# Shared expert's down products five steps late, expert blocks in plain fp32 products, and a block loop turned two ahead

## The reference, cut to what matters

```python
xt = x.reshape(-1, D)                                   # 1568 x 256, layer-normed
gates = softmax(xt @ Wg.T); scores, inds = top_k(gates, 2)
h = silu(xt @ We_gate[e].T) * (xt @ We_up[e].T)         # 16 experts, hidden 128
y = sum over the token's two experts of score * (h @ We_down[e].T)
shared = silu(xt @ Ws_gate.T) * (xt @ Ws_up.T) @ Ws_down.T   # hidden 512
out = x + y + sigmoid(xt @ Wsg.T) * shared
```

## Time and profile before

| | us |
|---|---|
| median of 3 runs | 531.88 |
| the runs | 524.18 to 536.82 |
| profiled execution, its own span | 541.3 |
| PE busy in it | 398.8 (74%) |
| DVE, ACT, POOL busy | 336.6, 198.6, 149.2 |
| embedding, attention, gate scores (to 347.8) | 347.8 |
| shared expert on PE (347.8 to 434.9) | 87.1 |
| expert blocks on PE (434.9 to 516.3) | 81.4 |
| last scatters, sum and store (516.3 to 541.3) | 25.0 |

### The profile page before, as it was taken

One profiled execution on the slowest core, in us unless ns is written; L12 is line 12 of the kernel. 1 busy time (PEld: TensorE's weight loads), 2 busy tenths in 40 slices (PEclk: granted clock), 3 DMA queues, 4 the chain that ended last, 5 costly groups with the idle time before them and its releaser, 6 DMA issues.

```text
span 541.3 us, 11594 instructions
## 1 busy us (share of the span) xinstructions
PE 398.8 (74%) x3554; PEld 354.9 (66%) x3555; DVE 336.6 (62%) x962; ACT 198.6 (37%) x569; POOL 149.2 (28%) x209
## 2 busy tenths in 40 slices
PE   4777768788897878878778885568686877887910
PEld 5766657677786767767667664567676877876800
DVE  2888842637677777778687775672635644444537
ACT  4433354314243334334342222330422445555600
POOL 2534441011112121212111112066740015445420
PEclk9899969958798989899998886589898999889865
DMA  7323445532615161625435010482230004343247
GB/s 249 89 72 86 158 57 103 69 57 46 118 41 115 46 119 43 101 60 91 79 53 120 9 50 0 174 345 67 74 112 14 1 20 133 93 125 112 72 126 231
DMA packets 50985, 50.48 MB, mean 93 GB/s; under 512 B 30442, under 2 KB 43502, under 8 KB 50816
## 3 DMA queue, kind: packets, MB, share of 16 engines
q1 hardware_dynamic: 46080, 38.25, 29.8%
q0 software_dynamic: 4864, 11.71, 7.0%
HBM read 23.59 MB, written 15.34 MB: 72 GB/s over the span
## 4 chain that ended last, share of the span: by engine, by line
issue 44%; PE 15%; DVE 12%; SPq 7%; POOL 6%; DMA 5%; another core or an unknown queue 5%; ACT 4%; POOLq 1%; DVEq 0%; ACTq 0%
PE bank L1081 8%; SPq L455 5%; PE pair L1081 2%; DMA Ks<-parts 2%; POOL picked L582 2%; POOL sq L535 2%; PE bank L1243 1%; DVE h L1071 1%; DMA wg_sb<-wg 1%; DMA picked<-by,bx 1%; DMA yt<-picked 1%; DVE h L1069 1%; ACT we_h L710 1%; DVE hs L1027 1%
## 5 line engine op out<-in xcount | busy, mean ns | idle before, releaser
L1167 PE MATMUL pair<-vx,PT 98*128 98x128 f32 x512 | 82.2, 311 | 32.4 <-DVE on L893 32.3
L1167 PEld LDWEIGHTS pair<-vx,PT 98*128 98x128 f32 x512 | 73.1, 220 | 37.6 <-ACT PT L668 29.8
L870 DVE TENSOR_REDUCE smax<-bank 128x8 f32<-128x392 f32 x64 | 36.0, 562 | 52.4 <-PE bank L1147 51.6
L582 POOL DMA_INDIRECT picked<-by,bx x40 | 39.3, 983 | 79.9 <-ACT by L752 63.3
L668 ACT ACTIVATE PT<-bank 98x512 f32<-98x512 f32 x64 | 38.2, 597 | 62.0 <-PE bank L1156 60.0
L535 POOL TENSOR_TENSOR sq<-att 128x256 f32<-128x256 f32 x16 | 9.7, 609 | 160.1 <-DVE att L903 160.1
L1156 PE MATMUL bank<-cs,Sm 128*98 128x128 f32 x256 | 44.6, 302 | 0.0
L576 POOL DMA_INDIRECT slots_x<-hn2x,slot_u x32 | 34.3, 1073 | 27.4 <-DVE slot_u L1001 17.9
L1092 PE MATMUL bank<-wt_h,x_h 128*98 128x256 f32 x96 | 29.9, 311 | 10.9 <-DVE wt_l L762 6.8
L1048 DVE TENSOR_TENSOR bxT_l<-bank,bxT_h 128x256 fp32r<-128x256 f32 x40 | 17.0, 425 | 30.3 <-ACT bxT_h L735 24.2
L877 DVE TENSOR_TENSOR Sm<-bank,smax 128x392 f32<-128x392 f32 x64 | 35.0, 548 | 1.2
(11 more groups left out here) (188 smaller groups left out, 1162.0 us busy)
## 6 DMA issues: line engine op xcount, KB each, us to landing
we_raw<-we SPq DMA_DIRECT2D x12, 512.0 KB, 7.3
slots_x<-pad POOLq DMA_DIRECT2D x8, 642.5 KB, 6.5
bx<-slots_x SPq DMA_DIRECT2D x40, 128.5 KB
xr<-xt SPq DMA_DIRECT2D x16, 294.0 KB, 2.8
Qs<-parts SPq DMA_DIRECT2D x96, 49.0 KB
Ks<-parts SPq DMA_DIRECT2D x96, 49.0 KB
vx<-vst SPq DMA_DIRECT2D x64, 52.1 KB
yt<-picked SPq DMA_DIRECT2D x16, 196.0 KB
```

What stands on the lines that cost most here:

```text
L582: G.indirect_dma_start(out=picked, out_offset=bass.IndirectOffsetOnAxis(ap=bx[b % BX][:].bitcast(U32)[:, D:ROW], axis=0), in_=by[b % 4][:] ...
L870: V.tensor_reduce(smax[b][:], s3, AX.X, ALU.max).then_inc(maxed, 1)
L1167: last = T.matmul(bank[4 + b][:, m * 2 * VN:(m + 1) * 2 * VN].rearrange("p (j n) -> p j n", j=2), PT[b][:, m, :], vx[n][:, :, h0:h0 + VN], ...
```

## The change

The shared expert is no longer cut in chunks. `shared_expert` runs 16 steps u (chunk u//4, quarter u%4) on every engine: gate and up of u, then the down product of tile u-5; five more steps do the last downs. `hs_h` and `hs_l` are double. The experts' weights are not split: they are loaded into `we_sb` and used as fp32, and so are the turned rows (`bxT`, 4 buffers) and `bhT`. A block's gate/up is then 2 plain fp32 matmuls of 256 columns instead of 6 fp32r ones, its down product 1 instead of 3. Rows are turned two blocks ahead instead of one. The copy of the result (`block_keep`) moves from ACT to DVE; `by` has eight buffers. POOL copies the row numbers to a small tile (`keep_id`) four blocks ahead of the scatter, and SP reloads a `bx` buffer as soon as its rows are turned and its numbers kept. PE's wait for all `sh_acc` ahead of the blocks becomes a wait in the first two `block_hturn`.

```diff
+        DOWN_LAG = 5
+        NU = NSH * SB
...
-            pipeline(eng, steps, NBLK, BX, 1, 2, BX, begin)
+            pipeline(eng, steps, NBLK, BX, 2, 2, BX, begin)
+
+        def shared_expert(eng, gate_up, down):
+            for u in range(NU + DOWN_LAG):
+                if u < NU:
+                    gate_up(u // SB, u % SB, u)
+                if u >= DOWN_LAG:
+                    down(u - DOWN_LAG)
...
             def load_block(b):
                 if b >= BX:
-                    sp.wait_ge(by_out[b % 4], 16 * ((b - BX) // 4 + 1))
+                    sp.wait_ge(b_turned, b - BX + 1)
+                    sp.wait_ge(id_kept, b - BX + 1)
...
+            pool.wait_ge(sh_u, NU)
+            def keep_id(b):
+                q = b % BX
+                pool.wait_ge(bx_in[q], 16 * (b // BX + 1))
+                need(pool, by_out[q], 16 * (b // BX))
+                G.tensor_copy(bid[q][:], bx[q][:].bitcast(U32)[:, D:ROW]).then_inc(id_kept, 1)
+            ID_LEAD = 4
...
             for b in range(NBLK):
+                if b + ID_LEAD < NBLK:
+                    keep_id(b + ID_LEAD)
...
-            def split_expert(n):
-                act.wait_ge(we_in[n], 16)
-                A.activation(we_h[:, n * STG:(n + 1) * STG], we_raw[:, n * STG:(n + 1) * STG], ACT.Copy).then_inc(w_hi, 1)
...
-            blocks(act, [(1, block_hi), (0, block_silu), (-1, block_hhi), (-2, block_keep)])
+            blocks(act, [(2, block_xT), (0, block_silu), (-1, block_hT)])
...
+            def block_keep(b, q):
+                dve.wait_ge(b_y, b + 1)
+                need(dve, by_out[q], 2 * b - 2 * q)
+                V.tensor_copy(by[q][:], bank[6 + q % 2][:, 0:D]).then_inc(b_ykept, 1)
+            blocks(dve, [(0, block_h), (-2, block_keep)])
...
+            def shared_down(t):
+                c, tt = divmod(t, SB)
+                pe.wait_ge(sh_lo, SB * c + SB)
+                need(pe, sh_acc, t - 1)
...
             def block_gu(b, q):
-                pe.wait_ge(b_lo, b + 1)
+                pe.wait_ge(b_xT, b + 1)
                 need(pe, b_h, b - 1)
-                product(bank[2 + par][:, 0:2 * HID], [(bxT_h[par][:, k, :], bxT_l[par][:, k, :],
-                                                       we_h[:, bass.ds(e + k * 2 * HID, 2 * HID)],
-                                                       we_l[:, bass.ds(e + k * 2 * HID, 2 * HID)])
-                                                      for k in range(KD)]).then_inc(b_gu, 1)
+                for k in range(KD):
+                    last = T.matmul(bank[2 + par][:, 0:2 * HID], bxT[q % 4][:, k, :], we_sb[:, bass.ds(e + k * 2 * HID, 2 * HID)],
+                                    start=(k == 0), stop=(k == KD - 1))
...
-                product(bank[6 + par][:, 0:D], [(bhT_h[par][:], bhT_l[par][:], we_h[:, bass.ds(e, D)],
-                                                 we_l[:, bass.ds(e, D)])]).then_inc(b_y, 1)
-            blocks(pe, [(1, block_turn), (0, block_gu), (-1, block_hturn), (-2, block_down)], begin=expert_weights)
+                T.matmul(bank[6 + par][:, 0:D], bhT[par][:], we_sb[:, bass.ds(e, D)], start=True, stop=True).then_inc(b_y, 1)
+            blocks(pe, [(2, block_turn), (0, block_gu), (-1, block_hturn), (-2, block_down)], begin=expert_weights)
```

More of the change, by code:

```diff
@@ L218, in build @@
         la = late.take
-        we_h = la("we_h", [128, WE], F32R)
-        we_raw = Zone(late.at, ceiling).take("we_raw", [128, WE])
-        we_l = la("we_l", [128, WE], F32R)
+        we_sb = la("we_sb", [128, WE])
         sgl = la("sgl", [128, SH])
         hs = la("hs", [128, SH])
-        hs_h = la("hs_h", [128, SB, SH], F32R)
-        hs_l = la("hs_l", [128, SB, SH], F32R)
+        hs_h = [la(f"hs_h{n}", [128, SB, SH], F32R) for n in range(2)]
+        hs_l = [la(f"hs_l{n}", [128, SB, SH], F32R) for n in range(2)]
         ma = Zone(late.at, ceiling).take
@@ L250, in build @@
         ba = Zone(kept.at, shared.at).take
-        bxT_h = [ba(f"bxT_h{n}", [128, KD, BLK], F32R) for n in range(2)]
-        bxT_l = [ba(f"bxT_l{n}", [128, KD, BLK], F32R) for n in range(2)]
+        bxT = [ba(f"bxT{n}", [128, KD, BLK]) for n in range(4)]
         bsg = [ba(f"bsg{n}", [BLK, HID]) for n in range(2)]
         bh = [ba(f"bh{n}", [BLK, HID]) for n in range(2)]
[L255 to L258, removed]
+        bhT = [ba(f"bhT{n}", [HID, BLK]) for n in range(2)]
+        by = [ba(f"by{n}", [BLK, D]) for n in range(BX)]
+        bid = [ba(f"bid{n}", [BLK, 1], U32) for n in range(BX)]
+        ya = Zone(shared.at, ceiling).take
+        yt = [ya(f"yt{n}", [TT, TOPK, YG, D]) for n in range(NT // YG)]
         bank = [ctx.enter_context(nc.psum_tensor(f"bank{n}", [128, 512], F32)) for n in range(4)]
@@ L306, in build @@
         scattered, ids_moved = sem("scattered"), sem("ids_moved")
[L307 to L308 removed]
+        wsh_in, we_in = sem("wsh_in"), sem("we_in")
+        wsh_hi, wsh_lo = sem("wsh_hi"), sem("wsh_lo")
         sh_g, sh_u, sh_silu, sh_h, sh_hi, sh_lo, sh_y, sh_acc = (
@@ L311, in build @@
         bx_in = [sem(f"bx_in{n}") for n in range(BX)]
-        b_turned, b_hi, b_lo, b_gu, b_silu, b_h, b_hturned, b_hhi, b_hlo, b_y, b_ykept = (
-            sem("b_" + n) for n in ("turned", "hi", "lo", "gu", "silu", "h", "hturned", "hhi", "hlo", "y", "ykept"))
-        by_out = [sem(f"by_out{n}") for n in range(4)]
+        b_turned, b_xT, b_gu, b_silu, b_h, b_hturned, b_hT, b_y, b_ykept = (
+            sem("b_" + n) for n in ("turned", "xT", "gu", "silu", "h", "hturned", "hT", "y", "ykept"))
+        by_out = [sem(f"by_out{n}") for n in range(BX)]
+        id_kept = sem("id_kept")
         y_in = [sem(f"y_in{n}") for n in range(NT // YG)]
@@ L492, in _ @@
                 load_block(b)
-            for q in range(4):
-                sp.wait_ge(by_out[q], 16 * NBLK // 4)
+            for q in range(BX):
+                sp.wait_ge(by_out[q], 16 * NBLK // BX)
             for g in range(NT // YG):
@@ L1042, in _, with shared_gate_up @@
-            for c in range(NSH):
-                shared_chunk(c)
-            def block_lo(b, q):
-                par = q % 2
-                dve.wait_ge(b_hi, b + 1)
-                V.tensor_tensor(bxT_l[par][:].rearrange("p k t -> p (k t)"), bank[par][:, 0:D],
-                                bxT_h[par][:].rearrange("p k t -> p (k t)").bitcast(F32), ALU.subtract).then_inc(b_lo, 1)
+            dve.wait_ge(padded, 16 * NT // 2)
+            def shared_gate_up(c, b, u):
+                dve.wait_ge(sh_silu, u + 1)
+                dve.wait_ge(sh_u, u + 1)
+                need(dve, sh_hi, u)
+                need(dve, sh_lo, u)
+                V.tensor_tensor(hs[:], sgl[:], bank[(2 * b + 1) % 4][:, 0:SH], ALU.mult).then_inc(sh_h, 1)
+                dve.wait_ge(sh_hi, u + 1)
+                need(dve, sh_y, 4 * (c - 1))
+                V.tensor_tensor(hs_l[c % 2][:, b, :], hs[:], hs_h[c % 2][:, b, :].bitcast(F32), ALU.subtract).then_inc(sh_lo, 1)
@@ new lines, in shared_down @@
+            def shared_down(t):
+                c, tt = divmod(t, SB)
+                rows = slice(tt * TT, (tt + 1) * TT)
+                pe.wait_ge(sh_lo, SB * c + SB)
+                need(pe, sh_acc, t - 1)
+                product(bank[4 + t % 2][0:TT, 0:D], [(hs_h[c % 2][:, b, rows], hs_l[c % 2][:, b, rows],
+                                                      wsh_h[:, SGU + b * D:SGU + (b + 1) * D], wsh_l[:, SGU + b * D:SGU + (b + 1) * D])
+                                                     for b in range(SB)]).then_inc(sh_y, 1)
```

123 lines of the change are left out of this document (41 added, 82 removed).

## The result

| | before | after |
|---|---|---|
| median | 529.38 us (4 runs, 524.18 to 536.82) | 514.17 us (4 runs, 507.41 to 515.9) |
| ratio, 95% interval | | 0.970 (0.960 to 0.979): faster |
| profiled execution, its span | 541.3 us | 513.0 us |

The account below looks back on a forecast made before the run. PE was taken to bound both changing stages, shared expert and expert blocks. Terms of -19.6 and +2.6 made -17, from a median of 531.9 to 515, stated as 516 us for fp32's upward room, range 503 to 529.

Parts of the forecast that it names:

- The standstills: Shared expert: PE's four waits between gate/up and downs all go with downs five steps late, -13.2 us.
- The clock: Time lost to PE's lowered clock: shared expert regains 4.8 of 7.8 us, blocks keep all 4.9.
- The late releases: Shared expert: PE's releases arrive late while POOL scatters; 5 of 6.6 us stay, -1.6.
- rival 1: Late releases eat the shared expert's gain: it gains 8 to 10, blocks lose 2.6, whole 525; chance 0.17.
- Splits worth nothing: Shared expert: dropping 12 ACT copies and 12 DVE subtractions (14.6 us) gains nothing beyond what is counted elsewhere.
- Plain fp32: Blocks: plain fp32 products cost PE 0.26 us more a block, +10.4 over 40; bounds +8 and +15.
- Register load: Blocks, loop top: 6.7 us of loading 16 registers stays, some of it covered, -2; bounds 0 and -5.
- Short gaps: Blocks: 5 of 6.5 us in ten PE gaps, most waiting for `bxT`, go through decoupling.
- `sh_acc`: Ahead of the blocks: PE's wait for the last `sh_acc` goes, -0.8 us.
- Rival 2: Block loop clearly longer: +9 instead of +2.6, or POOL's pace over 2 us; whole 522 to 524; chance 0.12.
- rival 4: PE's clock stays low in the block loop, 1.65 us more a block; whole over 542 up to 577; chance 0.05.
- Rival 3: Block loop shorter: its 14.2 us remainder shrinks by 9, register load by 5; whole 509; chance 0.16.

Follow-up runs that it names:

- e_chunk: Changed kernel with the shared expert in chunks again (four gate/ups, then four downs), double buffers kept, no splits of the experts' weights: 521.93 us, ratio 0.986.
- e_lag3: Changed kernel with the downs three steps late instead of five (`DOWN_LAG = 3`): 524.22 us, ratio 0.991.
- second profile of before: The kernel before, unchanged, measured and profiled again: 533.96 us, span 532.3.
- e_splits_chunk: Changed kernel with the shared expert in chunks and the twelve splits of the experts' weights put back into unread scratch buffers: 525.55 us, ratio 0.999.
- second profiles: Repeat profiles of both kernels, unchanged: the kernel before 533.96 us, the changed kernel 510.48 us (6 runs), ratio 0.967.
- e_splits_lag5: Changed kernel, downs still five steps late, with the twelve splits of the experts' weights put back into unread scratch buffers: 510.51 us, ratio 0.970.
- e_fp32r3: Changed kernel with each plain fp32 product of the blocks replaced by three fp32r matmuls of the same operands: 500.81 us, ratio 0.940.
- e_lead1_reload: Changed kernel with rows turned one block ahead instead of two and `bx` reloaded only after its block's scatter has landed: 513.81 us, ratio 0.972.
- e_fp32r1: Changed kernel with each plain fp32 product of the blocks replaced by one fp32r matmul, corrections left out: 492.9 us (one run).
- e_regs2: Changed kernel with the 16 offsets loaded eight at a time behind queued gate/ups, values taken again at the loop's top: 506.63 us (6 runs), ratio 0.965.
- second set of runs: The changed kernel, unchanged, measured again: 510.48 us (6 runs), ratio 0.967.

## Why the prediction was right, and where it was not

**The standstills (-13.2): mechanism right, size from an unusual execution.** That the downs wait for the last `hs_l` and that five steps remove it is shown by e_chunk and e_lag3. The second profile of before has 10.4 us, not 13.2, and 1.5 us of them belong to the splits (e_chunk 8.9). The double buffers have no part in it: e_splits_chunk has them and stands still for the same 10.4.

**The clock (-4.8 of 7.8, and -0 of 4.9): the term that was mis-sized most, in the blocks.** In the second profiles the loss in the blocks is 0.05 x 75.6 = 3.8 us before and 0 after, so 3.8 came back instead of 0. In the shared expert it is 0.12 x 78.6 = 9.4 us before and 0.04 x 60.2 = 2.4 after, 7.0 instead of 4.8, but that is less sure: e_splits_chunk, where PE has the same work and the same standstills as in the kernel before, lost only 0.07 x 74.9 = 5.2, and e_splits_lag5 0.05 x 62.1 = 3.1, which makes 2.1. The clock's part of this stage varies by 4 us between executions with the same waits.

The prediction kept the blocks' loss "since they follow these gaps", but the change made these gaps fewer and shorter. In the earlier trace rows the gaps of the loop top are 1.4 to 2.1 us among ten others; with 0.9 to 1.4 us (up to 1.6 in e_fp32r3), and at most two short ones beside them (e_lead1_reload), the clock was full from start to end of the blocks, in all of the profiles with those blocks that this study has. It was full in e_fp32r3 as well, so the plain fp32 products are not the reason. In e_fp32r1, with 1.8 to 2.2 us, it fell again (0.93). Even there it fell behind only two of the four gaps, and in the second profile of before behind the two of 0.81 and 1.36 us at the start and the one of 1.96, but not behind those of 1.53, 1.70 and 1.78. That the shorter gaps kept the clock up fits all profiles; no run changes the gaps and nothing else, so it is not shown.

**The late releases (5 of 6.6 kept): wrong, and so was rival 1.** Nothing in the kernel brings them about each time. The kernel before has them in one profile and not in the other, and no other kernel of the study has them, packed downs and splits or not (e_chunk, e_splits_chunk). What raised them is open, and so is how often they come. That this execution was 9 us above the median of its runs was known; the prediction used it to shift its sum, but did not ask which rows were those 9 us. The two stages took 87.1 + 81.4 = 168.5 us in it and 154.2 in the second profile: late releases, standstills longer by 2.8, and longer blocks.

**Splits worth nothing: right**, 62.1 against 62.0 us (e_splits_lag5). In chunks they cost 1.5 us.

**Plain fp32 (+10.4): right, 1.2 too much.** 0.218 us a record against 0.22, 0.23 us a block against 0.26, +9.2.

**Register load (-2 of 6.7): right.** 4.5 us are left. That they are on PE's path in the changed kernel is shown by e_regs2, which takes them away.

**Short gaps (-5 of 6.5) and `sh_acc` (-0.8): about right in the sum, not in what the gaps were.** All idle time of PE ahead of the turns fell from 12.0 us in the second profile of before to 4.8:

```profile
L1243 PE MATMUL bank<-cs,bx 128*128 128x128 f32 x80 | 16.8, 293 | 12.0 <-issue 8.0 <-DMA bx<-slots_x 3.0 <-DVE h L1039 0.8
```

The second profile of before has no gap that waits for `bxT` of the block just turned, which five of the ten behind the earlier trace rows did (five, not most, as the prediction has it). Its short gaps are six waits for the rows (3.0 us, one of them 1.70), and the change removed these. 8.0 us of "issue" are the four loop tops, 6.6 us, and one gap of 1.36 at the loop's start, which is gone too.

The blocks then add up: 75.6 + 9.2 (fp32) - 7.2 (these gaps) - 3.8 (clock) = 73.8; measured were 72.3 and 73.0, and the last 0.8 to 1.5 us are in waits within the blocks that were not taken apart. The predicted +2.6 was a measured -3.3; of the difference of 5.9 the clock is 3.8 and the fp32 term 1.2.

**The sum: right in part by luck.** Between the second profiles the two stages gain 18.4 + 3.3 = 21.7 us; the medians of this case differ by 15.2 to 18.4 (529.38 and 514.17; 528.85 and 510.48). Some of the 18.4 is the clock's luck: e_splits_chunk and e_splits_lag5 stand for the shared expert of before and after with 74.9 and 62.1 us, a gain of 12.8, and 12.8 + 3.3 = 16.1 is close to what the medians say. The part ahead of the stages, whose length varies by 17 us from run to run with the same code, leaves the rest open. The prediction's -17 was right for the whole because two errors went opposite ways. Its gain of the shared expert was too large (-19.6 for -12.8 to -18.4), since that stage was taken from an execution with late releases and longer standstills. And it left out the gain of the clock in the blocks (+2.6 for -3.3). Nothing in its reasoning made them cancel. The stage lengths that it forecast, 67.5 and 84, had no such luck: they were counted down from 87.1 and 81.4, which the second profile has as 78.6 and 75.6.

**The rivals.** Rival 2 and rival 4 are out: a block is 1.63 us, POOL's pace 1.34 and the clock full. Rival 4 also began from too much: even in the first profile the clock was full behind the loop top at 450.82 and fell only behind the other three. Rival 3 (509) came nearest by stages: the blocks did get shorter, and the second set of runs has 510.48. But it gave 5 us of the register load and 9 of the remainder as the reason, and the runs show 2.1 us of the load and 3.8 of the clock, which it does not name.

## What to carry to other kernels

Before a sum is built on a profile, compare its span with the other times: where it lies outside all of them, look for rows that other executions may not have (here idle time put down to no engine), or take a second profile. A product that consumes what the engines behind its neighbour have yet to finish needs whole further steps of work between the two; to alternate them is not enough. Three steps late was as slow as chunks, five removed every wait. Where a change takes gaps away, ask in the same term what becomes of the clock lost behind them: here all 3.8 us in the blocks came back.

## What the runs showed of the hardware

- A plain fp32 matmul of 256 columns is two records of 0.218 us. In place of three fp32r matmuls each, the three products of a block take 0.23 us more, a fifth of the 1.06 us of the fp32r ones.
- Loading 16 registers at a loop's top stops PE for 0.9 to 2.2 us each time (0.91 in the changed kernel, 2.19 in e_fp32r1), and no stop is left (e_regs2) when eight at a time stand behind work that is already queued.
- POOL's indirect scatter with one copy of 128 numbers beside it runs at 1.34 us, and the scatter alone at 1.28 to 1.29 (the last four of e_fp32r1).
- PE's releases reached the other engines up to 7 us late in one execution of a kernel and on time in another. Seen in one of thirteen profiles.
- The same code ahead of the shared expert took 342.7 to 359.9 us, at a mean granted clock of 0.90 in the shortest (e_splits_chunk) and 0.85 in the longest (e_lead1_reload).
